# A fused adaLN, attention and gated FFN kernel: the order of its first operations rewritten, three of block 0's element-wise steps moved from GpSimd to VectorE

## The reference

```python
# first part
scale, shift = split(cond @ W_emb + b_emb)
xn = rms_norm(x, g_norm) * (1 + scale) + shift         # x_square, x_norm, x_turn, x_scale, x_shift
q, k, v = heads(xn @ W_qkv)                            # a_qk, a_v
q, k = rms_norm(q, g_q), rms_norm(k, g_k)              # a_square, a_sum, a_rms, a_scale
o = softmax(q @ k.T / 4) @ v                           # a_scores, a_shift, a_exp, a_pv
r = o + o @ W_out                                      # r_mm
# second part
attn = causal_attention(rms_norm(r, ln1))              # b_...
mod = 0.1 * tanh(attn @ Wo.T @ A)                      # m_...
h = rms_norm(r, ln2)
gate = silu(h @ W_in.T + mod * (h @ A) @ B)            # f_gate
out = x + r + (gate * (h @ W_up.T)) @ W_down.T         # f_up, f_down
```

## Time and profile before

| | us |
|---|---|
| median of 3 runs | 649.42 (649.32 to 651.33) |
| profiled execution, its own time | 646.44 |
| its span, first to last instruction | 644.6 |
| PE busy | 600.9 (93%) |
| DVE busy | 462.1 (72%) |
| ACT busy | 370.0 (57%) |
| POOL busy | 221.1 (34%) |

### The profile page before, as it was taken

How to read it: one execution, slowest core, us unless ns; L and a number is a source line. 1 busy time by engine, 2 the same in 40 slices (tenths; PEclk the granted TensorE clock), 3 DMA queues, 4 the chain that set the end, 5 groups by cost and what they waited for, 6 DMA issues and landing times.

```text
span 644.6 us, 22549 instructions
## 1 busy us (share of the span) xinstructions
PE 600.9 (93%) x9112; PEld 558.6 (87%) x9128; DVE 462.1 (72%) x1070; ACT 370.0 (57%) x803; POOL 221.1 (34%) x196
## 2 busy tenths in 40 slices
...
DMA packets 31961, 24.35 MB, mean 38 GB/s; under 512 B 7632, under 2 KB 30800, under 8 KB 31872
## 3 DMA queue, kind: packets, MB, share of 16 engines
...
q10 hardware_dynamic: 544, 0.66, 0.4%
...
## 4 chain that ended last, share of the span: by engine, by line
PE 75%; SPq 10%; DVE 6%; issue 4%; ACT 2%; DMA 2%; POOL 1%; POOLq 0%; ACTq 0%; DVEq 0%
PE gate_bank L494 12%; PE up_bank L494 11%; PE down_bank L718 10%; SPq L469 10%; PE b_banks L494 7%; PE a_banks L486 7%; PE x_bank L486 6%; PE a_banks L609 4%; PE b_banks L486 3%; PE b_banks L506 2%; PE gate_bank L704 2%; PE a_banks L506 2%; PE up_bank L533 2%; DMA vj<-vs 2%; PE b_banks L671 2%
## 5 line engine op out<-in xcount | busy, mean ns | idle before, releaser
L1123 POOL TENSOR_TENSOR gl<-gu,gh 128x512 fp32r<-128x512 f32 x64 | 83.1, 1299 | 117.9 <-ACT gh L877 117.7
L1075 DVE SCALAR_TENSOR_TENSOR th<-th,gate_bank 128x512 f32<-128x512 f32 x64 | 43.2, 675 | 46.8 <-ACT th L872 46.8
L494 PE MATMUL up_bank<-uh,wup_hi 128*128 128x256 f32 x256 | 76.3, 298 | 0.0
L1111 POOL TENSOR_TENSOR qk<-qk,rx 128x512 f32<-128x512 f32 x32 | 33.3, 1060 | 123.6 <-DVE rx L903 123.6
L718 PE MATMUL down_bank<-wdn_hi,gh 128*128 128x256 f32 x256 | 74.1, 290 | 0.6 <-POOL gl L1123 0.6
L494 PE MATMUL gate_bank<-uh,win_hi 128*128 128x256 f32 x256 | 72.4, 283 | 0.2
L718 PE MATMUL down_bank<-wdn_hi,gl 128*128 128x256 f32 x256 | 72.1, 282 | 0.0
L718 PE MATMUL down_bank<-wdn_lo,gh 128*128 128x256 f32 x256 | 72.1, 282 | 0.0
L494 PE MATMUL up_bank<-ul,wup_hi 128*128 128x256 f32 x256 | 71.9, 281 | 0.0
L494 PE MATMUL up_bank<-uh,wup_lo 128*128 128x256 f32 x256 | 71.9, 281 | 0.0
L494 PE MATMUL gate_bank<-ul,win_hi 128*128 128x256 f32 x256 | 71.4, 279 | 0.0
...
## 6 DMA issues: line engine op xcount, KB each, us to landing
xa<-in_x SPq DMA_DIRECT2D x16, 256.0 KB, 3.6
xres<-in_x SPq DMA_DIRECT2D x16, 256.0 KB, 2.9
vj<-vs SPq DMA_DIRECT2D x256, 16.0 KB
out<-outb SPq DMA_DIRECT2D x16, 256.0 KB, 3.2
...
```

Source lines behind the costliest of these rows:

```text
L494: mm = pe.matmul(dst, w[a][:, k, c0:c0 + P], mov[b][:, k, :], start=(first and k == 0 and j == 0), stop=(last and k == KT - 1 and j == 2), ...
L1075: dve.scalar_tensor_tensor(out=whole, in0=whole, scalar=1.0, in1=Gb[:, :], op0=ALU.add, op1=ALU.mult).then_inc(f_half, 1)
L1111: pool.tensor_tensor(heads_of, heads_of, rx[:, 32 * t:32 * t + 32].unsqueeze(2).to_broadcast([P, 2 * H, HD]), ALU.mult).then_inc(done[name ...
L1123: pool.tensor_tensor(gl[:, c % 2], gu[:, c % 2], gh[:, c % 2].bitcast(F32), ALU.subtract).then_inc(f_lo, 1)
```

## The change

START begins differently. Behind `a_copy0` of block 1 the steps follow in the same order as before, but for some loads that have gone to the front and one `warm_down`. ORDER and END are the same. The parts:

1. SP's first transfers are x of block 0, the identity, both halves of W_qkv, then x of block 1; W_o, A and W_v follow before the load of piece 2. b_emb and g_norm are issued by ACT's queue.
2. For block 0 alone `x_shift`, `x_lo` and `a_scale0` are done by DVE. `a_scale1` stays on POOL.
3. On ACT hi 0 and hi 1 stand ahead of `x_norm` of block 0, both `a_square` ahead of both `a_copy`, and hi 2, `a_v_out`, hi 3 and hi 4 follow. On DVE lo 2 stands behind `a_rms` of block 0.
4. The pair `("warm", n)` now issues n matmuls of zeros. There were 36 in four places (15, 6, 9, 6); there are 26 in four (9, 8, 3, 6). A new `warm_down` issues 8 ahead of `a_pv` of block 0 and 6 behind `r_mm` of block 0, into another bank.

```diff
-    ("mt_zero", 0), ("ld_emb", 0), ("first_rms", 0), ("b_emb_one", 0), ("warm", 0), ("warm", 0), ("warm", 0),
...
+    ("mt_zero", 0), ("ld_emb", 0), ("x_load", 0), ("ld_ident", 0), ("ld_b_emb", 0), ("load", 0), ("load", 1),
...
+    ("a_rms", 0), ("m_mm", 0), ("a_v", 0), ("a_v_out", 0), ("hi", 3), ("lo", 2), ("a_scale0", 0), ("a_scale1", 0),
+    ("x_turn", 1), ("warm", 3), ("a_turn0", 0), ("a_turn1", 0), ("hi", 4), ("x_norm0", 1), ("x_norm1", 1),
...
+        def first(n):
+
+            return isinstance(n, int) and n == 0
...
                     pe.wait_ge(once["mt_zero"], 1)
-                    for _ in range(3):
-                        pe.matmul(Ub[0:96, 0:192], mt[:, 0, :], mt[:, :, :].rearrange("p t n -> p (t n)"), start=True, stop=True)
+                    for _ in range(n):
+                        pe.matmul(Ub[0:96, 0:192], mt[:, 0, :], mt[:, :, :].rearrange("p t n -> p (t n)"),
+                                  start=True, stop=True)
+                elif name == "warm_down":
+                    pe.wait_ge(once["scale_cols"], 1)
+                    for _ in range(n):
+                        pe.matmul(Db[0:96, 0:192], mt[:, 0, :], mt[:, :, :].rearrange("p t n -> p (t n)"),
+                                  start=True, stop=True)
...
+                elif name == "ld_b_emb":
+                    for col, v, k in ((0, b_emb, 4), (6, g_norm, 2)):
+                        with nc.allow_non_contiguous_dma(reason="vectors of features onto partitions"):
+                            act.dma_start(small[:, col:col + k], v.rearrange("(k p) -> p k", p=P)).then_inc(loaded["b_emb"], 16)
...
+                elif name == "x_shift" and first(n):
+                    dve.wait_ge(once["shift_cols"], 1)
+                    dve.wait_ge(done["x_scale"], 1)
+                    xmv = by_seq(xm[:, :, :])
+                    dve.tensor_tensor(xmv, xmv, shiftT[:, :, 0:SEQS].unsqueeze(3).to_broadcast([P, KT, SEQS, S]),
+                                      ALU.add).then_inc(done[name], 1)
+                elif name == "x_lo" and first(n):
+                    dve.wait_ge(done["x_hi"], 1)
+                    dve.tensor_tensor(al[:, :, :], xm[:, :, :], ah[:, :, :].bitcast(F32), ALU.subtract).then_inc(done[name], 1)
+                elif name == "a_scale0" and first(n):
...
+                if name in ("x_shift", "x_lo", "a_scale0") and first(n):
+                    return
```

More of the change, by code:

```diff
@@ L84 @@
-    ("hi", 11), ("a_shift0", 1), ("a_rowsum1", 1), ("b_v0", 0), ("load", 3), ("a_scale1", 2), ("a_scale0", 2),
-    ("a_rowsum0", 1), ("b_shift0", 0), ("b_shift1", 0), ("a_flip1", 1), ("a_flip0", 1), ("hi", 12), ("o_odd", 1),
-    ("load", 4), ("b_v1", 0), ("x_square", 3), ("b_scores", 0), ("o_hi", 1), ("load", 5), ("m_tanh", 0),
-    ("f_lo0", 0), ("x_load", 3), ("a_v", 1), ("x_turn", 2), ("load", 6), ("x_hi", 2), ("ld_causal", 0),
-    ("b_rowsum1", 0), ("b_rowsum0", 0), ("lo", 11), ("a_pv0", 1), ("a_pv1", 1), ("f_up0", 0), ("b_flip1", 0),
@@ L89 @@
-    ("b_flip0", 0), ("o_even", 1), ("x_scale", 2), ("o_lo", 1), ("r_square", 1), ("a_weigh0", 2), ("a_square0", 2),
-    ("a_weigh1", 2), ("load", 7), ("m_out", 0), ("r_norm1", 1), ("r_norm0", 1), ("lo", 12), ("a_copy1", 2),
-    ("load", 8), ("r_hi", 1), ("a_square1", 2), ("m_mul", 0), ("r_rms", 1), ("f_tanh0", 0), ("a_copy0", 2),
-    ("b_k_out1", 1), ("a_sum0", 2), ("r_add", 1), ("r_lo", 1), ("a_sum1", 2), ("b_pv", 0), ("r_mm", 1),
[8 rows of a table removed]
-    ("r_load", 0), ("r_turn", 1), ("b_rowsum0", 1), ("o_even", 2), ("o_odd", 2), ("a_scale1", 3), ("f_gate0", 0),
[4 rows of a table removed]
@@ L106 @@
-    ("m_tanh", 1), ("load", 12), ("a_copy0", 3), ("a_copy1", 3), ("m_out", 1), ("f_lo1", 1), ("x_load", 4),
-    ("b_move", 0), ("a_weigh0", 3), ("vd_zero", 0), ("r_square", 2), ("x_norm0", 4), ("x_norm1", 4), ("a_rms", 3),
-    ("f_up2", 0), ("a_v", 2), ("f_gate3", 0), ("r_load", 1), ("x_turn", 3), ("f_down0", 0), ("f_up3", 0),
-    ("b_weigh1", 2), ("f_down1", 0), ("a_pv0", 2), ("a_pv1", 2), ("a_qk1", 3), ("r_rms", 2), ("a_qk0", 3),
-    ("f_half0", 1), ("f_out", 0), ("b_pv", 1), ("x_lo", 4), ("f_down2", 0), ("r_lo", 2), ("f_tanh0", 1),
[13 rows of a table removed]
@@ new lines @@
+    ("emb_shift", 0), ("scale_cols", 0), ("x_turn", 0), ("x_scale", 0), ("shift_cols", 0), ("x_shift", 0),
+    ("warm", 8), ("x_hi", 0), ("lo", 1), ("x_lo", 0), ("ld_wo_a", 0), ("ld_wv", 0), ("load", 2), ("x_load", 2),
[4 rows of a table added]
+    ("lo", 3), ("mblk", 0), ("g_col", 0), ("x_scale", 1), ("hi", 5), ("x_square", 2), ("warm", 6), ("a_scores", 0),
[7 rows of a table added]
+    ("r_norm0", 0), ("b_k", 0), ("r_hi", 0), ("a_rms", 1), ("r_rms", 0), ("b_q", 0), ("v2_lo", 0), ("a_q_out", 1),
[7 rows of a table added]
+    ("a_flip0", 1), ("hi", 12), ("o_odd", 1), ("load", 4), ("b_v1", 0), ("x_square", 3), ("b_scores", 0),
@@ new lines @@
+    ("o_hi", 1), ("load", 5), ("m_tanh", 0), ("f_lo0", 0), ("x_load", 3), ("a_v", 1), ("x_turn", 2), ("load", 6),
+    ("x_hi", 2), ("ld_causal", 0), ("b_rowsum1", 0), ("b_rowsum0", 0), ("lo", 11), ("a_pv0", 1), ("a_pv1", 1),
+    ("f_up0", 0), ("b_flip1", 0), ("b_flip0", 0), ("o_even", 1), ("x_scale", 2), ("o_lo", 1), ("r_square", 1),
+    ("a_weigh0", 2), ("a_square0", 2), ("a_weigh1", 2), ("load", 7), ("m_out", 0), ("r_norm1", 1), ("r_norm0", 1),
+    ("lo", 12), ("a_copy1", 2), ("load", 8), ("r_hi", 1), ("a_square1", 2), ("m_mul", 0), ("r_rms", 1),
[11 rows of a table added]
```

28 lines of the change are left out of this document (16 added, 12 removed), and 94 rows, old and new, of the table START.

## The result

| | us |
|---|---|
| before, median of 21 runs | 648.99 (644.19 to 652.55) |
| changed kernel, median of 21 runs | 651.32 (649.52 to 652.77) |
| ratio to before, 95% interval | 1.0043 (1.0023 to 1.0062) |
| profiled execution after, its own time and its span | 651.38, 649.6 |

The change makes the kernel slower by 0.43%. The ratios in this document leave out executions more than 1.5% above the fastest of the same kernel; the medians are over all. The forecast was 650.1 us and called "no change" likelier than "slower". The spread changed too. The fastest half of the runs of before lies from 644.19 to 648.99 us.

A forecast was written before the change was run, and what follows sets the result against it. Before 88 us one dependency thread through all engines was taken as the bound, after it TensorE. +2.8 us at the scores and -2.1 by the clock gave +0.7 on 649.42, so 650.1 us, range 646.0 to 653.3.

The forecast's parts named there:

- no change: Whole kernel: time within about 0.3% (1.95 us) of before, chance 0.51; slower had 0.32 and faster 0.17.
- The sum: Whole kernel: +2.8 us at the scores, -2.1 by the clock, together +0.7 us.
- A: Load of W_k holds ACT and the clock holds over `a_pv`: 650.1 us, own range 648.8 to 651.6; chance 0.46.
- B: Same stall as A, but the clock falls between the zeros and `a_pv`: 652.2 us; chance 0.31.
- The head: Up to `a_qk` of block 0: earlier x and two steps on DVE gain about 4 us.
- The second part: From `a_qk` to `a_rms` of block 0: another 0.8 us gained, `a_rms` ending near 20.9 us.
- The third part: Late lo 2 delays the load of W_k, which holds ACT: of 4.8 us gained, 0.2 remain at `x_turn` of block 1.
- The fourth part: Zero matmuls and low clock on TensorE: scores 2.8 us later, then 2.1 us back at `a_pv` and `a_qk` of block 1.
- the 2.1 us of clock: TensorE at full clock: `a_pv` 1.76 instead of 2.42 us, `a_qk` of block 1 3.03 instead of 4.37.
- about a microsecond either way: Allowance for later falls of the clock, such as the one that made 24 matmuls slow, in any case.

The follow-up runs named there:

- kernel 1: The changed kernel with hi 2 and lo 2 moved ahead of block 0's squares: 647.24 us, ratio to before 0.9975; repeated on another chip 647.44 us, 0.9976.
- Experiments 1 to 3: kernel 1; the changed kernel with hi 4 behind `x_norm` of block 1, 1.0003; the kernel before with lo 2 and lo 3 behind `a_rms` of block 0, 1.010.
- Experiment 7: The changed kernel with 16 instead of 8 zero matmuls ahead of `a_pv` of block 0 and four more behind it: 651.65 us, ratio to before 1.0068.
- Before again: The kernel before, text unchanged, run and profiled once more on a further chip: median 648.42 us, profiled execution 650.90 us.
- "again" profiles: The kernel before and the changed kernel, texts unchanged, each profiled once more on one further chip: medians 648.42 and 652.02 us, ratio 1.0036.
- kernels 5: The changed kernel without the eight zero matmuls ahead of `a_pv` and the six behind `r_mm` of block 0: 655.26 us, ratio to before 1.0131.
- Kernel 6: The changed kernel with the shift and the lo of block 0 back on POOL: 659.45 us, ratio to before 1.0193.
- kernel 8: kernel 1 with TensorE's gaps filled by zero matmuls around `a_pv`, `x_turn` and later transposes: 647.88 us, ratio 1.0013; repeated on another chip 646.76 us, 0.9961.

## Why the prediction failed where it did

By its number the forecast came near: 651.32 us against 650.1. Part of that is luck. The sum said +0.7 us, the medians differ by 2.3 and the two profiled executions by 5.0. And the time alone does not tell A from B: 651.32 lies inside A's own range and 0.9 below B's 652.2.

**The head.** `a_qk` of block 0 started at 14.14 us, 13.5 forecast, inside the 13 to 14.5 named. ACT started on x at 4.46 (4.6 taken), 0.30 us behind its own table load. The two steps on DVE took 0.69 and 0.68, as priced.

**The second part.** 1.4 us between `a_qk` and `a_rms` (17.2 to 18.57), as forecast; `a_rms` ended at 21.59, 0.7 later, by the later start.

**The third part, on which all rested, held.** Load behind lo 2 (22.22, forecast 22.0), idle ACT of 4.87 us (forecast some 4), `x_turn` at 27.59, at the late end of the 26 to 27.6. Its sum comes to 26.7, not 26.6, and two of its terms were off and cancel in part: lo 2 took 0.69, not 1.1, and ACT could use the load 3.57 us after its issue (22.22 to 25.79), not 2.9. The rule of the Trainium skill (GPSIMD Engine Reference, "Specifications") on collisions of POOL and DVE shows in the next row: `a_scale0`, two inputs in SBUF, took 1.55 us beside POOL's `a_scale1`, against 0.69. lo 2 overlapped POOL for 0.45 us and was not stretched. What I had missed is which of the two starts first. lo 2 started 0.24 us ahead of POOL's `a_scale1`, and `a_scale0` 0.37 behind it. In kernel 1 `a_scale0` starts 0.05 us ahead of POOL's `a_scale1` (22.12, 1.56 us) and runs wholly beside it, unstretched:

```profile
22.07 0.69 DVE L1035 TENSOR_TENSOR qk<-qk,rx 128x512 f32<-128x512 f32 x1
```

It is so in all profiles of changed kernels: 1.54 or 1.55 us in the seven where POOL started first, 0.69 in the four where DVE did. Before as well: the 0.95 us piece was not alone, as I took it, but started at 13.58, 0.10 ahead of POOL's shift; the 1.80 us one started while it ran. That `a_scale0` gains nothing on DVE was right. Experiments 1 to 3 show the stall.

**The fourth part.** The sequence came as priced: 1.09, 2.13, `a_turn` ended at 31.7 (31.5), the scores at 35.02 (34.8), `a_pv` at 42.77 (42.6) and 1.77 us. The term that failed is the last: "the twelve of `a_qk` of block 1 take 3.03 instead of 4.37". They took 5.41. My rule was that a gap of 2.0 us keeps the clock and one of 3.3 loses it, and I asked of the 2.9 us ahead of `a_pv` only whether the clock would last until `a_pv` began. In this profile it lasted until `a_pv` ended, and fell there; in the second profile of the same kernel it fell at 43.4, just as `a_pv` began. What I left out is that the 64 small matmuls need not keep the clock up. Experiment 7, which fills the gaps ahead and behind, gets the 3.0 us. So the 2.1 us of clock were 0.65 gained at `a_pv` less 1.04 lost at `a_qk`, a net loss of 0.4.

**What I had no term for.** Behind it W_k and W_q of block 1 took 5.40 instead of 4.85 and `r_mm` of block 1 2.90 instead of 1.62. I had allowed "about a microsecond either way". From +3.0 at the scores the profile goes to +3.4 at W_k, +5.7 at `r_turn` of block 1 and +5.0 at the end, not +0.7. Also, START does have work behind 88 us, contrary to what I wrote (`r_turn` of block 2, at 132.4 us, is one of its steps); the part that was rewritten lies ahead of it.

**The baseline.** About half of these 5.0 us come from the execution of before that was profiled first: at 646.44 us it lay 2.55 below its median. Before again shows three slow chains with nothing changed. Both "again" profiles are from one chip and have nearly the same three chains (5.47, 5.49 and 2.65 or 2.79 us). Between them `x_turn` is 0.1 us later in the changed kernel, the scores 2.3, `r_turn` of block 1 1.9, of block 2 0.9, the end 1.3. So the part of the change that does not hang on the clock's pattern is the later scores, and the clock terms of my sum are zero in this pair.

How the patterns are spread can be read from the mean clock of each run. The 81 runs of before in the ratios of the experiments, on three chips, fall into three groups: 33 runs at 0.972 to 0.974 with a median of 645.7 us, 19 at 0.965 to 0.968 with 647.8, 29 at 0.963 and below with 650.7. My two profiles of before are one of the first group and one of the last (0.960). The changed kernel, 0.965 to 0.971 in all its first 21 runs, has a median of 651.3: some 3.5 us above the runs of before with a like mean clock (on the chip of the "again" rows alone 652.0 against 648.4). So the low clock by itself does not make the difference. The mean does not tell in which chains the low stretches lie, and the middle group of before was not profiled.

**By the rivals**, the first profile has A's sign (`a_pv` 1.77) and the second B's (2.42), of one program; the medians (+2.3 us) are nearer B's +2.8 than A's +0.7. The stall was common to both. I gave A 0.46 and B 0.31 as if one of them had to hold in every execution.

**Open.** From `r_turn` of block 2 to the end it takes 511.2 to 513.9 us in ten profiles, and 515.6 to 517.1 in four (kernels 5, 6, 7, and 8 on the further chip), though the text is the same there. So the premise that a lead at the early steps reaches the end held to within 2 us in the ten and failed by 3 to 5 in the four. For kernel 8 the waits on x explain a part. Kernel 6 has five waits of 0.98 us ahead of `r_turn`, in every second block, where the others have one or none. What puts an execution into the longer form was not found. It is part of why kernels 5 and 6 cost more than their early part says, and why kernel 7 gains nothing.
